# New positions for every task of a one-core attention and mixture-of-experts kernel, later small loads, and filler matmuls from a list

## What is computed

```
q, k, v = x @ Wq.T, x @ Wk.T, x @ Wv.T              # 16 heads of 8
attn    = softmax(causal(q k.T * 8**-0.5))
x       = layernorm(x + (attn v) @ Wo.T)
scores  = sigmoid(x @ router.T)                     # 64 experts in 8 groups
...                                                 # 4 groups by their two best, then 8 experts
coef    = 2.5 * chosen scores / their sum           # zero for the others
h       = silu(x Wg[e]) * (x Wu[e]) * coef[:, e]    # 64 wide for each expert
x       = layernorm(x + sum_e h Wd[e] + silu(x SWg) * (x SWu) @ SWd)
```

## Time and profile before

| quantity | value |
|---|---|
| executions | 956.84, 956.91, 958.35 us |
| span of the profiled execution | 952.6 us |
| instructions in it | 16050 |
| TensorE busy | 932.2 us (98%) |
| VectorE busy | 750.5 us (79%) |
| GpSimd busy | 598.4 us (63%) |
| ScalarE busy | 462.6 us (49%) |
| moved by DMA | 121.70 MB |

### The profile page before, as it was taken

The page is one execution under the profiler, slowest core; times in us unless marked ns, Lnnn a source line. Parts: engine busy times, 40 slices in busy tenths (PEclk is TensorE's granted clock), DMA queues, the critical chain, the costliest instruction groups (busy, mean ns, idle before and its releaser), DMA issues.

```text
span 952.6 us, 16050 instructions
## 1 busy us (share of the span) xinstructions
PE 932.2 (98%) x5008; PEld 581.8 (61%) x5008; DVE 750.5 (79%) x2374; ACT 462.6 (49%) x866; POOL 598.4 (63%) x651
## 2 busy tenths in 40 slices
PE   8899999999999999999999999999999999999996
PEld 3355566666666666666666666675666666666664
DVE  5776887799877997799967997699967996578664
ACT  3355455455555545555555545555545555533221
POOL 2342247775777657775767757776667767775653
PEclk9799999999999999999999999999999999999998
DMA  8552154334534253433534254242633323242431
GB/s 292 159 167 67 50 176 146 113 104 136 181 96 135 92 184 126 136 114 96 192 115 136 84 179 138 94 136 73 211 117 113 114 88 95 87 162 82 138 129 56
DMA packets 64340, 121.70 MB, mean 128 GB/s; under 512 B 6656, under 2 KB 36224, under 8 KB 63744
## 3 DMA queue, kind: packets, MB, share of 16 engines
q1 hardware_dynamic: 64256, 120.67, 39.6%
HBM read 98.37 MB, written 22.02 MB: 126 GB/s over the span
## 4 chain that ended last, share of the span: by engine, by line
PE 85%; DVE 9%; issue 2%; DMA 2%; ACT 1%; SPq 0%; POOL 0%; POOLq 0%; DVEq 0%; ACTq 0%
PE acc L879 12%; PE ob L820 7%; PE sm L790 7%; PE st L808 7%; PE pu L749 6%; PE pg L749 5%; PE pg L751 5%; PE pg L750 5%; PE pu L750 5%; PE pu L751 5%; PE acc L745 4%; PE acc L864 2%; PE acc L866 2%; PE acc L865 2%; PE ob L832 2%
## 5 line engine op out<-in xcount | busy, mean ns | idle before, releaser
L993 POOL TENSOR_TENSOR hid<-hid,coef_b 128x512 f32<-128x512 f32 x240 | 309.5, 1290 | 134.7 <-DVE hid L1250 106.0
L1182 DVE CUSTOM_DVE_ANT_0 max_out<-sm,causal_sb 128x128 bf16<-128x128 f32 (+3 forms) x512 | 236.1, 486 | 60.6 <-PE sm L790 58.6
L942 ACT ACTIVATE hid<-pg 128x512 f32<-128x512 f32 x243 | 145.3, 598 | 245.2 <-PE pg L751 236.6
L914 ACT ACTIVATE probs<-st 128x512 f32<-128x512 f32 (+1 forms) x384 | 192.5, 525 | 75.8 <-PE st L808 74.1
L1241 DVE SCALAR_TENSOR_TENSOR hid<-hid,pg 128x512 f32<-128x512 f32 x243 | 165.8, 682 | 51.1 <-ACT hid L942 50.8
L997 POOL TENSOR_TENSOR hid_lo<-hid,hid_hi 128x512 fp32r<-128x512 f32 x112 | 144.0, 1285 | 75.7 <-ACT hid_hi L949 75.3
L1250 DVE TENSOR_TENSOR hid<-hid,pu 128x512 f32<-128x512 f32 x235 | 160.3, 682 | 30.0 <-PE pu L751 27.8
L979 POOL TENSOR_SCALAR_AFFINE_SELECT probs<-probs 128x256 f32<-128x256 f32 x256 | 97.8, 408 | 75.3 <-ACT probs L914 75.3
L790 PE MATMUL sm<-k_stack,q_stack 72*128 72x128 bf16 (+3 forms) x512 | 132.8, 307 | 3.7 <-DMA k_stack<-k_rows_dram 1.9
L749 PE MATMUL pg<-x_hi,wg_hi 128*128 128x512 f32 x240 | 127.7, 532 | 0.3 <-DVE hid L1241 0.2
L808 PE MATMUL st<-q_stack,k_stack 96*128 96x512 bf16 (+3 forms) x512 | 125.9, 304 | 0.2
(11 more groups left out here) (161 smaller groups left out, 1295.4 us busy)
## 6 DMA issues: line engine op xcount, KB each, us to landing
coef_b<-coef_dram SPq DMA_DIRECT2D x128, 512.0 KB, 3.9
q_rows_dram<-qk_parts SPq DMA_DIRECT2D x24, 384.0 KB, 4.1
k_rows_dram<-qk_parts SPq DMA_DIRECT2D x24, 384.0 KB, 3.5
q_stack<-q_rows_dram SPq DMA_DIRECT2D x64, 144.0 KB
k_stack<-k_rows_dram SPq DMA_DIRECT2D x64, 144.0 KB
xT_sb<-in_xT SPq DMA_DIRECT2D x8, 256.0 KB, 3.8
y<-in_x SPq DMA_DIRECT2D x8, 256.0 KB, 3.9
out<-out_sb SPq DMA_DIRECT2D x8, 256.0 KB, 2.6
```

The lines of the kernel that those rows point to most:

```text
L914: act.activation(probs[:, h % HG, at:at + wide], st_bank[i % 2][:, 0:wide], ACT.Exp, scale=C ** -0.5).then_inc(exp_done, 1)
L942: act.activation(hid_of(n, i), gate_bank(n, i)[:, :], ACT.Tanh, scale=0.5).then_inc(tanh_done, 1)
L993: pool.tensor_tensor(hid_of(n, i), hid_of(n, i), coef_b[:, half % 2, j, :], ALU.mult)\
L1182: last = dve.tensor_tensor_reduce(out=max_out[:, seg.nth(BANK_SM, task) % 2, col:col + wide], in0=sm_of(seg, task)[:, col:col + wide], in1 ...
```

## The change

1. **Positions.** All nine tables of positions get new numbers. Every table differs; one line of the old and one of the new are shown.
2. **Fillers.** The rule is replaced by a list `FILLS` of tasks with the number of fillers in front of each. There are 8 + 138 fillers now and 8 + 62 + 170 before.
3. **Small loads.** They leave `rs` 1 and become two tasks of their own, `wsm` 0 (four small weights) and `wsm` 1 (1 MB of Wd). The waits move to their users: `oproj` of sequence 0 and `d` of unit 2.
4. **New waits on the weights' low parts** before four expert tasks and before the first two loads of coefficients, and one of the first `g` on all earlier `sm` banks.
5. Names that leave the value as it was (`IN_PROBS` is 3, `sm_banks` returns 2), so banks and buffers are the same.

```diff
 FIRST = {
-    "ld": (-76.7507,),
-    "q": (-50.93722,),
+    "ld": (-118.38366,),
+    "q": (-73.74117,),
...
-FILL = dict(mx=1, st=1, tk=1)
-FILL_BEFORE, FILL_START = 8, 62
+FILL_BEFORE = 8
+FILLS = {("v", 0, 0): 7, ("mx", 0, 0): 52, ("mx", 0, 2): 2, ("mx", 0, 4): 2, ("mx", 0, 5): 1, ("mx", 0, 6): 1,
...
+    ("mx", 1, 26): 1, ("mx", 1, 27): 2, ("x1T", 0, 0): 1, ("mx", 1, 29): 1, ("router", 0, 0): 4, ("st", 1, 12): 2,
+    ("st", 1, 16): 1, ("st", 1, 18): 1, ("st", 1, 20): 2, ("st", 1, 23): 2, ("coefT", 0, 0): 3}
...
         small = [(wo_sb, woT), (rw_sb, rwT), (bias_sb, bias.unsqueeze(0).to_broadcast([P, E])),
-                 (sd_sb, SWd), (wd_sb, Wd[:, PAIRS // 2 * D:])]
+                 (sd_sb, SWd)]
...
-                    if kind == "rs" and (n, i) == (0, 1):
+                    if kind == "wsm" and i == 0:
                         for dst, src in small:
                             sp.dma_start(dst[:, :], src).then_inc(w_in, 16)
+                    if kind == "wsm" and i == 1:
+                        sp.dma_start(wd_sb[:, :], Wd[:, PAIRS // 2 * D:]).then_inc(wdown_in, 16)
...
+                        if n == 0 and i < 2:
+                            sp.wait_ge(lo_done, CHUNKS - SPLIT_BY_DVE)
...
-            first_expert = ALL.tasks.index(("g", 0, SHARED))
-            head = {t: FILL[t[0]] for t in ALL.tasks[:first_expert] if t[0] in FILL}
-            head[("v", 0, 0)] = FILL_START
+            half_units = PAIRS // 2 + 1
+            low_ready = {("g", 0, 1): 2, ("g", 0, half_units): 4, ("u", 0, half_units): 6, ("d", 0, 1): CHUNKS - 1}
...
-                    fill(head.get(before, 0))
-                    before = task = (kind, n, i)
+                    task = (kind, n, i)
+                    fill(FILLS.get(task, 0))
...
-                    if kind == "k" and n == 0:
+                    if kind in ("k", "v") and n == 0:
                         pe.wait_ge(wkv_in, 16 * 2)
-                    if kind == "pv" and (n, i) == (0, 0):
+                    if kind == "oproj" and n == 0:
                         pe.wait_ge(w_in, 16 * len(small))
...
+                    if (kind, n, i) in low_ready:
+                        pe.wait_ge(lo_done, low_ready[kind, n, i] + 1 - SPLIT_BY_DVE)
...
+                        if (n, i) == (0, 0):
+                            pe.wait_ge(sm_free, early)
...
+                            if (n, i) == (0, 2):
+                                pe.wait_ge(wdown_in, 16)
```

More of the change, by code:

```diff
@@ new lines @@
+    "ldtok": (-17.31818,),
+    "attT": (-18.44851,),
+    "oproj": (-17.24612,),
+    "ln": (-16.74636, -16.45566, -16.19383,),
+    "x1": (-16.0377, -15.86689, -15.86679, -15.74625,),
+    "x1T": (-13.93844,),
+    "router": (-13.51171,),
+    "tk": (-12.94618, -12.84198, -12.70048, -12.70038, -12.68202, -12.68192, -12.68182, -12.626, -12.6259, -12.60975,
+        -11.49473, -11.49463, -11.36791, -11.29181, -9.10025, -8.9906, -7.57708, -6.68588, -6.26085, -4.91141,),
+    "coefT": (-3.33162,),
@@ L151 @@
-    "coefT": (0.23127,),
-    "c": (1.23222, 1.39144,),
+    "ld": (-77.9707,),
+    "q": (-73.15321,),
+    "qsplit": (-72.11207, -70.24267,),
+    "k": (-69.28058,),
+    "ksplit": (-67.80929, -67.80919,),
[14 rows of a table added]
+    "mask": (-51.11243, -49.16155, -48.44419, -46.0881, -46.088, -45.92934, -45.67783, -45.18987, -30.34864,
+        -26.55725, -26.55715, -24.80754, -17.83372, -16.12449, -13.14487, -12.30274,),
+    "pv": (-44.21227, -32.47863, -21.43413, -13.67899,),
+    "ot": (-39.73308, -31.21949, -16.9038, -12.5657,),
@@ new lines @@
+    "on": (-37.96659, -25.10483, -16.61493, -11.46425,),
+    "ldtok": (-34.2886,),
+    "attT": (-10.83387,),
+    "oproj": (-9.55549,),
+    "ln": (-9.1524, -8.81923, -8.81913,),
+    "x1": (-8.45209, -8.35248, -7.83974, -7.83964,),
+    "x1T": (-7.14108,),
+    "router": (-5.37666,),
+    "tk": (-5.67007, -5.16625, -4.66679, -4.03823, -3.79735, -3.67539, -3.67529, -3.61068, -3.61058, -3.61048,
+        -3.01503, -2.42578, -2.1475, -2.06862, -1.5521, -0.02449, 0.03536, 0.0456, 0.19038, 0.50652,),
@@ L188 @@
-    "coefT": (0.70899,),
-    "c": (0.93334, 1.02101,),
+    "ld": (-85.82289,),
+    "q": (-68.91919,),
+    "qsplit": (-67.19876, -64.96987,),
+    "k": (-64.54769,),
+    "ksplit": (-61.29782, -57.8575,),
[14 rows of a table added]
+    "mask": (-42.36584, -41.65199, -39.21468, -35.79179, -30.10253, -29.85657, -27.86836, -27.56502, -24.92435,
+        -23.39537, -22.31501, -22.31491, -16.58448, -13.23339, -13.23329, -13.23319,),
+    "pv": (-36.29931, -29.08293, -21.7241, -14.29341,),
+    "ot": (-35.95189, -25.73162, -19.78252, -13.37444,),
@@ new lines @@
+    "on": (-33.3491, -22.36408, -17.36805, -11.54622,),
+    "ldtok": (-10.33681,),
+    "attT": (-10.05155,),
+    "oproj": (-9.64126,),
+    "ln": (-9.06741, -9.06731, -8.81388,),
+    "x1": (-7.69517, -7.69507, -7.53532, -7.49564,),
+    "x1T": (-6.68446,),
+    "router": (-5.88683,),
+    "tk": (-5.95139, -5.78298, -5.78288, -5.40573, -5.30022, -4.32572, -4.32562, -4.07756, -3.97192, -3.63989,
+        -3.31122, -2.89469, -2.5356, -2.44966, -2.44956, -1.03424, -1.02224, -0.60141, -0.47092, -0.42267,),
@@ L227 @@
-    "coefT": (0.24595,),
-    "c": (1.00056, 1.13375,),
+    "ld": (-71.25769,),
+    "q": (-63.67379,),
+    "qsplit": (-63.43538, -62.94333,),
+    "k": (-62.85982,),
+    "ksplit": (-62.53027, -62.03178,),
[14 rows of a table added]
+    "mask": (-41.98689, -39.71919, -39.71909, -37.62153, -30.95232, -30.46236, -30.07075, -29.85542, -22.82017,
+        -22.82007, -22.70012, -22.367, -15.04889, -13.97099, -13.93689, -13.93679,),
+    "pv": (-37.24563, -29.50519, -21.78062, -14.29582,),
+    "ot": (-36.64241, -27.30987, -18.76311, -11.73879,),
@@ L592, in bank_free, with sm_banks @@
                 eng.wait_ge(s, n)
+        early = sum(t[0] in BANK_SM for t in ALL.tasks[:ALL.tasks.index(("g", 0, SHARED))])
+        early_bank = (sm_bank[0], sm_bank[1], pg, pu)
+        def sm_banks(seg, task):
+            return 2
         def sm_of(seg, task):
-            return sm_bank[seg.nth(BANK_SM, task) % 2]
+            many = sm_banks(seg, task)
+            return early_bank[seg.nth(BANK_SM, task) % many]
         def for_dve(task):
```

151 lines of the change are left out of this document (51 added, 100 removed), and 348 rows, old and new, of tables (EXPERTS, EXPERTS_FIRST, EXPERTS_LAST, EXPERTS_SECOND).

## The result

| | us |
|---|---|
| before, median of 4 executions | 957.63 (956.84 to 958.47) |
| changed kernel, median of 4 | 948.57 (947.09 to 949.54) |
| ratio | 0.9913, 95% interval 0.9892 to 0.9934 |
| profiled execution of the changed kernel: span, time | 947.8, 949.54 |

The change takes 9 us, 0.9%. The forecast was 945, with a range from 930 to 957: the direction and most of the size came, and the rest of this document is about the 3.6 us between, behind which stand larger errors that partly cancel.

The account below looks back on a forecast made before the run. The kernel was taken as one long TensorE queue, with fillers the only excess between first `st` and `x1T`. Terms 5.2 - 0.4 - 10.2 - 3.5 + 2.3 - 1.9 - 3.1 = -11.6 from 956.9 gave 945.3 us, range 930 to 957.

Parts of the forecast that it names:

- start, to the first `mx`: Opening: mask lands later, TensorE stands some 5 us before `k`, first `mx` at 28.0 instead of 22.79; +5.2 us.
- first `mx` to first `st`: Stretch of 14.38 us before: VectorE's 11.7 us of work at 84% busy gives 14.0 us; -0.4 us.
- first `st` to `x1T`: Stretch of 64.34 us: fillers fall from 115 to 40, VectorE at 84% busy gives 54.1 us; -10.2 us.
- `x1T` to `coefT`: Stretch of 19.48 us: less VectorE work, still 88% busy, gives 16.0 us; -3.5 us.
- `coefT` to the first split `d`: Stretch of 11.68 us: Wd's low parts on GpSimd delay the first coefficient load to 5.9 us after `coefT`; +2.3 us.
- work done: By the first split `d`, one more `g`, `u` and `v` done, two `st` and one `mx` part fewer; -1.9 us.
- the full part: After the first split `d`: most of TensorE's waits for the negated maxima go, thanks to longer cover before `mT`; -3.1 us.
- The first rival: All removed fillers were on TensorE's path, 94 x 0.218 = 20.5 us, and the 3.1 go: 933 us; chance 0.13.
- The gap of 4.3 us: Median of executions, 956.9 us, lies 4.3 above the profiled span; taken as unchanged, differences summed from 956.9.
- The clock rival: With fewer fillers TensorE's clock stays at half between first `st` and `x1T`: slower, 987 us if throughout; chance 0.08.
- The waits as rival: TensorE waits where fillers stood, so the two stretches from first `st` to `coefT` stay 64.3 and 19.5 us: 959 us; chance 0.12.

Follow-up runs that it names:

- the two runs on the start: Changed kernel with v, the second megabyte weight load and Wg's low part moved back: 942.88 us; with only v moved back: 943.65 us.

## Why the prediction was right, and where it was not

| step | predicted | in the traces |
|---|---|---|
| start, to the first `mx` | +5.2 | +7.3 |
| first `mx` to first `st` | -0.4 | +0.5 |
| first `st` to `x1T` | -10.2 | -9.8 |
| `x1T` to `coefT` | -3.5 | -3.1 |
| `coefT` to the first split `d` | +2.3 | +2.3 |
| after it: work done (-1.9) and the full part (-3.1) | -5.0 | -2.1 |
| sum | -11.6 | -4.8 |

- **The mechanism was right, its size in part lucky.** The fillers between first `st` and `x1T` cost time, and with most of them gone the stretch is 9.8 us shorter, near the forecast's 10.2. The run with the old filler rule gives 11.7 back there. The first rival (all on the path) falls by those 0.154 us per filler. But the 10.2 came from VectorE at 84%, read from a window in which TensorE is busy throughout, and such a window shows no limit of VectorE. In the changed kernel VectorE is at 82% there and TensorE at 96%. What sets the 54.5 us was not isolated; that the forecast is within 0.4 of it does not show that VectorE does.
- **The start was mis-sized,** +7.3 for +5.2. The mask, v's evacuation and the start of `k` came within half a microsecond of the steps; the stand before `k` is 5.85 us for some 5, because `q` was done sooner. Missed was that `k`, after the stand, runs at the half clock: 2.08 us where 0.9 was put (which the earlier trace rows does not show either: 1.31 for q, 1.02 for k). All later steps of the split come about 1.5 us late, its last one ends at 22.3 for 20.8. The rest is the stack: issued 1.0 us late, it landed 3.3 us after its issue where 2.2 was put. That the delay passes to the end was assumed, and shown by the two runs on the start.
- **First `mx` to first `st`** was sized by VectorE at 84% too. In the run with eleven more fillers VectorE reaches 96% there, so the 84% was no limit of VectorE. The stretch holds half clock before and after, and after it also a wait of 2.0 us for `max_parts` (0.9 before), which the sum did not have; without it the stretch would have been shorter than the forecast's. The number came out near by luck.
- **`coefT` to the first split `d`** has the right number for a wrong reason. The load was late by about what was put (5.45 us after `coefT` for 5.9), but TensorE stands only 0.6 us of the stretch (busy 13.45 of 14.01); the stretch is long because it holds more matmuls (86 for 74). The -1.9 for work done was these same matmuls.
- **The full part, -3.1, failed,** though its mechanism was shown. From `coefT` of sequence 3 to that of sequence 7 the new tables take 422.3 us for 424.6, -2.3, and the waits for `max_parts` after 133 us are 0.4 us for 3.1. But sequences 0 to 3, where the tables differ from the repeated ones, take 324.3 us for 321.7, +2.6, of which the sum had 0.4 (+2.3 and -1.9). That they would cost nothing was taken over from the repeated part and not worked out. TensorE stands 1.8 us in them for 0.2 before, and the trace has waits for 1.5 of it: 0.6 for the loaded maxima, 0.4 for `max_parts` and 0.5 for the row maxima. The other 1.0 us is busy time, with the number of matmuls the same to within two; what it is was not isolated, since the tables can't be exchanged there without a seam.
- **The gap of 4.3 us** between span and median was taken as unchanged; the changed kernel's is 1.7. The traces' -4.8 and this -2.6 make the 7.4 between 956.9 and 949.54, and the profiled execution was the slowest of four. So against this pair of traces the terms were 6.8 us too hopeful, and against the medians, 957.63 and 948.57, 2.5: before's profiled execution was some 2.5 us better than its median and the changed kernel's 1 us worse than its own, and the rest is that the sum set out from 956.91.
- **The clock rival** (0.08) showed itself in the run of the changed order without later fillers: 27 us at half in one piece, from before the first `st` on, and 11 us on the time. With the chosen list it did not come. **The waits as rival** are part of it: with no filler left, TensorE waited where they had stood.

## What to carry to other kernels

A filler that keeps TensorE's clock is worth its place only where the engine would else wait; past that each one costs, here 0.154 us of its 0.218. Try none, all and a part. Here, with before's order, none was 0.3% slower than all. With the new order all was 1.5% slower than before, none 0.3% slower, and 41 in the long stretch where the old rule has 117 gave 0.9%. A busy share is a limit only if it was read where that engine was the one that held the others up. In the opening of a kernel, before its bound engine is full, most of what is lost goes to the end, so an early operation must not wait for a late load, and a load moved back in a queue has to be followed to whoever now stands behind it. Compare a profiled span with the time of its own execution, not with a median of others.
